# Queries computed by dimension in the first self-attention, and a low-rank down product moved into the next batch of the first feed-forward

## The reference

```python
def _L0_attn_ref(x, Wq, Wkv, Wkvh, Wg, Wout):      # H = 16 heads, D = 128
    q = (x @ Wq.T).reshape(b, n, H, D)
    ...                                             # k, v from kv and gated kv_head
    q, k = rope(q), rope(k)     # [t1*cos - t2*sin, t2*cos + t1*sin] over halves of D
    scores = where(tril, einsum('bnhd,bmhd->bhnm', q, k) * scale, -inf)
    o = einsum('bhnm,bmhd->bnhd', softmax(scores), v).reshape(b, n, H * D)
    return o @ Wout.T

def _L0_ffn_ref(x, gate_w, w_up, w_gate, w_down, up_A, up_B, gate_A, gate_B, down_A, down_B):
    topw, sel = top_k(x @ gate_w.T, 2)              # two of eight experts for each token
    for e in range(8):                              # H = 1408, rank 16
        c = ...                                     # weight of expert e for the token
        h_e = silu(base_up + lo_up) * (base_gate + lo_gate)
        ch = c[:, None] * h_e
        mixed_h += ch
        lora_down += 2 * (ch @ down_A[e].T @ down_B[e].T)
    return mixed_h @ w_down.T + lora_down
```

## Time and profile before

| what | value |
|---|---|
| median of 3 runs | 3221.95 us (3218.62 to 3222.39) |
| the profiled execution's own time | 3220.54 us |
| its span (first to last instruction) | 3218.7 us |
| busy: PE, DVE, ACT, POOL | 2812.4, 2067.4, 1768.8, 1464.8 us |
| mean granted TensorE clock | 0.962 of 2.4 GHz |
| `attn0` | about 0 to 703 us of the span |
| `ffn0` | about 1240 to 1854 us |

### The profile page before, as it was taken

The page is one execution under the profiler, slowest core; times in us unless marked ns, Lnnn a source line. Parts: engine busy times, 40 slices in busy tenths (PEclk is TensorE's granted clock), DMA queues, the critical chain, the costliest instruction groups (busy, mean ns, idle before and its releaser), DMA issues. The chain is left out here.

```text
span 3218.7 us, 64393 instructions
## 1 busy us (share of the span) xinstructions
PE 2812.4 (87%) x24738; PEld 1994.4 (62%) x24738; DVE 2067.4 (64%) x4863; ACT 1768.8 (55%) x3780; POOL 1464.8 (46%) x1555
## 2 busy tenths in 40 slices
PE   5999999967888887999999978888999999975787
PEld 3666666644666665777777756666666766753343
DVE  6677777767777765655555547766555565555886
ACT  4555555546888884333333257765444444454896
POOL 3444444435888884544444425551111122212686
PEclk8999999988999987999999989999999999997899
DMA  5000000001000013000000011002001110012000
GB/s 172 27 1 2 1 1 1 1 9 35 2 2 2 2 48 94 27 8 8 1 1 1 1 50 41 21 2 76 14 28 39 40 40 1 1 62 80 23 21 27
DMA packets 47125, 81.75 MB, mean 25 GB/s; under 512 B 5731, under 2 KB 15973, under 8 KB 46693
## 3 DMA queue, kind: packets, MB, share of 16 engines
q1 hardware_dynamic: 46820, 77.64, 7.4%
HBM read 73.44 MB, written 4.19 MB: 24 GB/s over the span
## 5 line engine op out<-in xcount | busy, mean ns | idle before, releaser
L1146 POOL TENSOR_TENSOR c_pT<-c_prob,c_pT 128x512 f16<-128x512 f32 x256 | 293.7, 1160 | 64.6 <-ACT c_pT L1096 63.3
L2029 POOL TENSOR_TENSOR c_prob<-c_prob,c_inv 128x512 f32<-128x512 f32 x128 | 133.4, 1044 | 302.6 <-DVE c_inv L2247 302.6
L789 DVE SCALAR_TENSOR_TENSOR a_pT<-psT,a_kvh_t,a_pT 128x256 f16<-128x256 f32 (+1 forms) x256 | 94.6, 411 | 169.2 <-ACT a_pT L695 169.2
L1339 ACT ACTIVATE c_prob<-psT 128x512 f32<-128x512 f32 x256 | 156.4, 611 | 72.5 <-PE psT L1268 52.8
L1146 POOL TENSOR_TENSOR a_pT<-a_prob,a_pT 128x384 f16<-128x384 f32 x128 | 120.8, 950 | 157.8 <-ACT a_pT L1096 157.4
L1423 DVE TENSOR_REDUCE c_peak<-psS 128x2 f32<-128x512 f32 x256 | 167.1, 683 | 13.5 <-PE psS L1249 11.4
L1096 ACT CAST c_pT<-c_prob 128x512 f16<-128x512 f32 x256 | 160.1, 626 | 0.0
L488 POOL TENSOR_TENSOR a_q_rot<-a_q_cos,a_q_sin 128x512 f32<-128x512 f32 x64 | 86.8, 1357 | 159.6 <-DVE a_q_sin L808 159.6
L2163 ACT ACTIVATE c_prob<-c_prob,c_negmax 128x256 f32<-128x256 f32 x256 | 128.1, 502 | 56.0 <-DVE c_negmax L2239 55.0
L507 POOL TENSOR_TENSOR a_prob<-a_prob,a_inv 128x128 f32<-128x128 f32 x128 | 52.6, 411 | 221.6 <-DVE a_inv L782 221.6
L1679 POOL TENSOR_TENSOR f_ch<-f_h,f_c 128x256 f32<-128x256 f32 x88 | 76.4, 868 | 142.3 <-DVE f_h L1896 142.3
(11 more groups left out here) (626 smaller groups left out, 11341.0 us busy)
## 6 DMA issues: line engine op xcount, KB each, us to landing
c_feed<-in_L_ffn_w1T SPq DMA_DIRECT2D x16, 512.0 KB, 3.7
c_feed<-in_L_ffn_w2T SPq DMA_DIRECT2D x16, 512.0 KB, 3.7
x_all<-in_x SPq DMA_DIRECT2D x8, 512.0 KB, 7.0
a_ring<-in_L_attn_WqT SPq DMA_DIRECT2D x8, 512.0 KB, 5.7
a_ring<-in_L_attn_WoutT SPq DMA_DIRECT2D x8, 512.0 KB, 4.0
a_feed<-in_L_xattn_Wq SPq DMA_DIRECT2D x8, 512.0 KB, 3.8
c_feed<-in_L_xattn_Wo SPq DMA_DIRECT2D x8, 512.0 KB, 4.4
c_feed<-in_L_ffn_w3T SPq DMA_DIRECT2D x8, 512.0 KB, 3.6
```

The lines of the kernel that those rows point to most:

```text
L789: last = dve.scalar_tensor_tensor(pT[1][:, r, m, m * P:N], T[:, m * N + m * P:(m + 1) * N], kvh_t[:, b % 2, m, H + h:H + h + 1], pT[0][:, ...
L1146: pool.tensor_tensor(pT[1][:, c % NPH, :], prob[:, c % NPX, :], pT[0][:, c % NPH, :], ALU.subtract)\
L1339: act.activation(prob[:, c % NPX, :], ST[c % 2][:, 0:EW], ACT.Exp).then_inc(s.e_done, 1)
L2029: pool.tensor_tensor(prob[:, h % NPB, :, :], prob[:, h % NPB, :, :], inv[:, h % NPB, :].rearrange("p (n a) -> p n a", a=1).broadcast_to([P ...
```

## The change

In `attn0` the queries are made by dimension. The weights of one head are now the stationary operand and the 256 tokens of `xT` the moving one, so that the product comes out already turned (128 dimensions by 256 tokens), two heads each time. `turn_q` goes, with its use of the `TB` banks, the ACT copy and the DVE subtraction out of that bank. In their place ACT copies `q_rot` to `qT[0]` one step after `AT_Q`, behind `hi_p`, and POOL subtracts for `qT[1]` in that step, behind `weigh`. The rotation now exchanges the halves of the partitions: its sine products are two instructions of 64 partitions by 512 elements instead of 128 by 256. The table `rope_q` is turned on the host. `scores` waits for the two heads' low part (`q_lo`).

In `ffn0` the products of `zs` by `dB` of batch `b-1` move behind `base(0)` of batch `b`; the additions and measurements move into steps `i` = 0 and 1 of DVE's loop, the normalization into `i` = 2, and POOL's root behind the first tile of its loop. The last batch keeps the old order.

```diff
-    TURN_Q, TURN_P, PV, WO, NORM = 2, 2, 3, 5, 21
+    SPLIT_Q, TURN_P, PV, WO, NORM = 1, 2, 3, 5, 21
...
 # attn0, POOL
+                def low_q(b, j):
+                    no = 8 * b + j
+                    pool.wait_ge(s.q_hi, no + 1)
+                    pool.tensor_tensor(qT[1][:, 2 * j:2 * j + 2, :], heads2(q_rot[:, no % 2, :]),
+                                       qT[0][:, 2 * j:2 * j + 2, :], ALU.subtract).then_inc(s.q_lo, 1)
...
                         weigh(head(t, 1))
+                    for b, j in due(t, AT_Q, SPLIT_Q):
+                        low_q(b, j)
                     for b, j in due(t, AT_Q):
                         add_q(b, j)
 # attn0, PE
-                def turn_q(b, j):
-                    no = 8 * b + j
-                    pe.wait_ge(s.q_ready, no + 1)
-                    T = turn_bank(("q", b, j))
-                    turn(("q", b, j), [(T[:, i * P:(i + 1) * P], q_rot[:, no % 2, i * P:(i + 1) * P])
...
                 def queries(b, j):
...
-                    for k in range(KE):
-                        last = three(pe, bank(key)[:, :], xT[0][:, r, k, rows], xT[1][:, r, k, rows],
-                                     wq[0][:, k, cols], wq[1][:, k, cols], k == 0, k == KE - 1)
+                    for i in range(2):
+                        cols = slice((2 * j + i) * D, (2 * j + i + 1) * D)
+                        for k in range(KE):
+                            last = three(pe, bank(key)[:, i * N:(i + 1) * N], wq[0][:, k, cols], wq[1][:, k, cols],
+                                         xT[0][:, r, k, :], xT[1][:, r, k, :], k == 0, k == KE - 1)
...
 # attn0, ACT
-                    for b, j in due(t, AT_Q, TURN_Q):
-                        c, n = divmod(j, NT)
-                        turned(("q", b, j), qT[0][:, c * HC:(c + 1) * HC, n * P:(n + 1) * P])
...
                         hi_p(head(t, TURN_P))
+                    for b, j in due(t, AT_Q, SPLIT_Q):
+                        no = 8 * b + j
+                        act.wait_ge(s.q_ready, no + 1)
+                        act.copy(qT[0][:, 2 * j:2 * j + 2, :], heads2(q_rot[:, no % 2, :])).then_inc(s.q_hi, 1)
 # attn0, DVE, rotate_q
-                    dve.tensor_tensor(cos, ps, rope_q[:, 0, n:n + 1, :].broadcast_to([P, HC, D]), ALU.mult)
...
+                    dve.tensor_tensor(cos, ps, rope_q[:, 0:1, :].broadcast_to([P, 2, N]), ALU.mult)
+                    dve.tensor_tensor(sin[0:half], ps[half:D], rope_q[half:D, 1:2, :].broadcast_to([half, 2, N]), ALU.mult)
+                    dve.tensor_tensor(sin[half:D], ps[0:half], rope_q[0:half, 1:2, :].broadcast_to([half, 2, N]), ALU.mult)\
...
-                        low(("q", b, j), qT[1][at], qT[0][at])
 # ffn0, POOL
+                        if t == 0 and b:
+                            for n in range(NT):
+                                rstd_on_pool(pool, s, b - 1, n, G)
 # ffn0, PE
+                def low_rank_down(b):
+                    after(pe, s.z_parts, b, 1)
+                    has_weights(b, "dB")
+                    for n in range(NT):
+                        at = slice(n * P, (n + 1) * P)
+                        three(pe, Y[n][:, :], zs[0][:, at], zs[1][:, at], dB[0][:, 0, :], dB[1][:, 0, :], False, True)\
+                            .then_inc(s.y_ready.handle, 1)
...
                     base(0)
+                    if b:
+                        low_rank_down(b - 1)
...
 # ffn0, DVE
+                        if b and i < NT:
+                            measure(b - 1, i)
+                        if b and i == NT:
+                            for n in range(NT):
+                                normalize(dve, s, b - 1, n, G)
...
-                    for n in range(NT):
-                        add_and_measure(dve, s, b, n, Y[n][:, :], s.y_ready, G, steps)
-                    for n in range(NT):
-                        normalize(dve, s, b, n, G)
```

More of the change, by code:

```diff
@@ L424, in turns @@
         def turns(t):
-            out = [("k", b, i) for b, i in due(t, AT_K)] + [("q", b, i) for b, i in due(t, AT_Q, TURN_Q)]
+            out = [("k", b, i) for b, i in due(t, AT_K)]
             if head(t, TURN_P) is not None:
@@ L1644, in ffn0 @@
         s.y_ready = sc.counter("y_ready", NT)
-        s.chain = sc.counter("chain", 1 + 2 * NT + 2 + 3 + 3 + NT * LN_STEPS)
+        s.chain = sc.sem("chain")
         s.pool_chain = sc.counter("pool_chain", 1 + TH_)
@@ L1837, in _, with step, measure @@
             def _(dve):
+                chained = [0]
+                def step(ins):
+                    chained[0] += 1
+                    ins.then_inc(s.chain, 1)
+                    dve.wait_ge(s.chain, chained[0])
+                def measure(b, n):
+                    after(dve, s.y_ready, b, n + 1)
+                    step(dve.tensor_tensor(G.r[:, n, :], Y[n][:, :], G.x[:, b * NT + n, :], ALU.add))
+                    step(dve.bn_stats(G.stats[:, n, :], G.r[:, n, :]))
+                    dve.memset(G.junk[:, :], 0.0)
+                    step(dve.bn_aggr(G.mv[:, n, :], G.stats[:, n, :]))
+                    dve.tensor_scalar(G.ve[:, n:n + 1], G.mv[:, n, 1:2], EPS, None, ALU.add)\
+                        .then_inc(s.var_ready.handle, 1)
                 dve.wait_ge(consts, 32)
@@ L1871, in _ @@
                     after(dve, s.mask_ready, b, 1)
-                    steps.done(dve.tensor_tensor(dmask[:, :], mask[:, 1, :], mask[:, 0, :], ALU.subtract))
+                    step(dve.tensor_tensor(dmask[:, :], mask[:, 1, :], mask[:, 0, :], ALU.subtract))
                     after(dve, s.act_a_ready, b, 1)
```

75 lines of the change are left out of this document (32 added, 43 removed).

## The result

The changed kernel takes 3199.31 us (median of four runs, 3195.58 to 3202.87) against 3222.17 for the kernel before (four runs): a ratio of 0.9934, 95% interval 0.9920 to 0.9949. It is some 23 us faster. The forecast was 3180 us: the sign was right, the size about half, and the time lies at the edge of the range, where rival B stood (3199).

The account below looks back on a forecast made before the run. PE was taken to bound `attn0` and `ffn0`, with a DVE-ACT ring pacing plain steps after the change. Gains of 27 + 5 + 10 = 42 us from 3220.5, plus 1.4, gave 3180 us; range 3163 to 3200.

Parts of the forecast that it names:

- rival B: The ring costs more, or `ffn0`'s DVE work delays its tile loop: 23 us gained, 3199 us; chance 0.17.
- PE's side: `attn0`: without query transposes and their turn-bank wait, PE alone needs 8.50 us for two plain steps instead of 9.26.
- the ring: `attn0`: DVE and ACT alternate from `rowmax` to next `rowmax`; lengthened from 7.89 to 8.70 us, it paces plain step pairs.
- rival A: PE stays the bound throughout, rotations cheap or more slack: 0.60 a place, 56 us gained, 3166 us; chance 0.19.
- The step that failed: `attn0`, per batch: three pairs with next-batch PE work gain 0.44 us each, the pair behind the gates none.
- the wait of 0.68 us behind the gates: `attn0`: PE already waits there for ACT's exponentials, so that pair of steps was forecast to gain nothing.
- attn0, the start: PE no longer stands in `turn_q` until POOL has added, but DVE has little to give: 5 us gained, bounds 0 and 9.
- 59 places in that regime: `attn0`: 59 of 64 places gain at the steady batch's rate, 59 / 8 x 3.6 = 27 us.
- ffn0: PE's wait for `zs` goes in seven of eight batches, 10.9 us, less 1.0 given back: 10 us gained.
- The 1.0 us given back: `ffn0`: `measure` delays the second product with `sil`, so PE waits some 0.15 us in each of seven batches.
- POOL at nothing: `attn0`: POOL's new `low_q`, taking it from 35.76 to 46 us a batch, costs nothing, hidden by slack.
- rival C: Slower: POOL takes over as the bound in `attn0`, up to 3245 us; chance 0.05.

Follow-up runs that it names:

- the last kernel: Changed kernel with sine products and the measurement of the batch before moved between `invert` and `lo_p`, copy and subtraction a step later: 3164.75 us, ratio 0.9834 to before.

## Why the prediction was half right

- **PE's side** was right. Its own time for a plain pair is 8.51 us (8.50 forecast), and the wait for a turn bank went. With the ring out of the way a batch shrinks by 80.75 - 75.51 = 5.24 us, 0.65 a place; rival A had 0.60. The change did free the PE time that it seemed to free.
- **The ring in plain pairs**: 8.67 us (8.70 forecast), but by two errors that cancel. The odd half is 291.12 - 285.79 = 5.33 us instead of 5.20, as the rotation grew by 0.85 and not 0.56 (0.29 for later starts), less 0.16 that DVE had waited for the queries ahead of it (from `lo_p` to the cosine product 0.82 us before, 0.66 now). The even half is 8.67 - 5.33 = 3.34 instead of 3.50, as the copy added 0.1 and not 0.25.
- **The step that failed** is "three that carry PE work for the next batch ... at 0.44, and none for the pair behind the gates". I priced the ring in plain steps alone and took PE's gain for the others. Measured: steps 2 and 3 lost 0.16, 4 and 5 gained 0.41, 10 and 11 lost 0.01, together 0.24 for the 1.32 forecast. Steps 6 and 7 lost 0.94 for a forecast of 0. Steps 8 and 9, which I counted as plain, gained 0.13 instead of 0.56. With the three plain pairs (1.80 instead of 1.68) this makes 1.23 instead of 3.56 us a batch.
- What made steps 6 and 7 lose is shown by taking parts away one at a time: measures out of step 5, 1.57 us back (the normalizations, behind the gates, leave step 6 with them); copy out of step 6, 0.51; half of the sine products, 0.52. Rotation, measures and copy stand in one chain ahead of the gates' exponentials, and before the change that part of the chain had slack. PE and ACT in step 6 of the kernel before, then the first product of step 6 and `hi_p` in the kernel after (its next rows on ACT stand above, at 254.59 and 255.10):

```profile
251.69 0.22 PE L117 MATMUL psS<-a_kT,a_qT 128*128 128x128 f16 x1
...
257.16 0.73 ACT L695 ACTIVATE a_pT<-psT,a_kvh_t 128x256 f16<-128x256 f32 x2
258.58 0.38 ACT L742 ACTIVATE a_g_abs<-psO 32x256 f32<-32x256 f32 x1 [0.69 <-PE psO L119]
...
247.25 0.22 PE L117 MATMUL psS<-a_kT,a_qT 128*128 128x128 f16 x1
...
253.98 0.73 ACT L697 ACTIVATE a_pT<-psT,a_kvh_t 128x256 f16<-128x256 f32 x2
```

Before, ACT waits 0.69 us for PE's gates product. That is the slack of everything ahead of it: a rotation longer by 0.59 us left steps 6 and 7 as they were. Counted from start to start it is 0.81 us (258.58 - 257.16, less the 0.61 by which the next instruction follows `hi_p` in the kernel after). The change puts 0.85 us of rotation and 0.51 of copy there (254.59 to 255.10), and PE, whose step 5 is 0.41 us shorter, comes to step 6 sooner by as much; now ACT comes last. From the step's first product to the gates' first instruction on ACT it was 258.58 - 251.69 = 6.89 us and is 255.10 - 247.25 = 7.85. The sum, 0.85 + 0.51 + 0.41 - 0.81 = 0.96, is that difference, and it is the loss of 0.94 to within 0.02. What follows, to the scores of step 8, is unchanged (264.29 - 258.58 = 5.71, and 260.79 - 255.10 = 5.69).

- So the wait of 0.68 us behind the gates, which I read as "no gain there", told of the work behind the gates' product. It told nothing of the work ahead of it, which had slack, but less than the change used up.
- **attn0, the start**: 5 us forecast, bounds 0 to 9. By the second batch's inputs the changed kernel was 3.8 us ahead (64.53 instead of 68.32), by the third's (150.69 instead of 153.55) 2.9. The longer rotations are what it lost: with 0.59 us more a rotation the kernel before lost 5.4 us by that place, and with half the sine products the changed one gained 3.7. DVE had to give what little it had, as the prediction said, but the price of its own new work was not in the 5.
- **59 places in that regime** was too simple as well: from the last batch's inputs to the end, with no next batch to cover DVE's measures, it is 146.5 us, 0.5 more than before (557.3 to 703.3).
- **ffn0**: the removed wait was right (10.9 us in seven batches; 12.4 - 0.7 = 11.7 measured). The 1.0 us given back did not show: 0.04 us a batch and not 0.15. The cost of measurements, roots and normalization at nothing fits this. Term: 12.3 instead of 10; the 0.6 between 11.7 and 12.3 I can't place.
- **POOL at nothing** was right to within a few tenths of a microsecond a batch in the steady steps; rival C had no ground. **Rival B** came true in its number, and its reason, a ring that costs more, was the right one, though the excess was in the crowded steps and not in every pair.

Left open: why the stage between, the first cross-attention, differs by up to 5 us from one profiled execution to another (617.5 to 622.3 us from the end of `attn0` to the first `zs`), in kernels that don't differ there; and why the granted clock falls behind some of the waits and not behind others.

The 0.46 us that PE still waits behind the gates in the last kernel is ACT's own work. From the gates' first instruction at 243.37 us to the end of the exponentials ACT is never idle, and two loads of its function tables are part of that:

```profile
244.21 1.28 ACT L754 ACT_TABLE_LOAD   x1
246.19 1.28 ACT L711 ACT_TABLE_LOAD   x1
248.45 0.23 PE L117 MATMUL psS<-a_kT,a_qT 128*128 128x128 f16 x1 [0.46 <-ACT a_prob L713]
```

## What to carry to other kernels

When a change takes work from the engine that binds and gives work to others, follow the chain between the others through *every* kind of step, not only through the plain ones, and find in each the place where an engine of that chain still waits for the one that binds. What is added ahead of it is free up to about the length of that wait (0.69 us here); beyond it, whatever is added is paid, and things that were free before are paid along with it. Then look on the loaded engine for the place in the step where it waits anyway, here between `invert` and `lo_p`: the same instructions in other places gave 35 us.

## What the runs showed of the hardware

- A DVE product takes 0.69 us for 512 elements of a partition on 128 partitions and 0.67 to 0.69 us on 64; halving the partitions saves nothing.
- Consecutive DVE instructions of 512 elements start 0.59 to 0.61 us apart when they begin on the same partition, and 0.69 to 0.73 apart when input or output begin elsewhere.
- Two DVE normalizations with one SBUF tensor each take 0.99 us by themselves and 1.83 us beside a POOL subtraction of 1.33 us.
- A load of ACT's function tables takes 1.28 us, and two of them stand in the work on the gates of every batch.
- Behind the same wait of 1.72 us, PE's granted clock was 0.50 for 3.3 us in one batch of the changed kernel and 1.00 in another.
